# Two attention blocks, a gated MLP and a cross-attention with two norms, 16 batches: packing the heads tile to tile, affine parts of two norms at the transposes, new step orders

## What is computed

```
h  = x + attention(rmsnorm(x), rmsnorm(x))           # "sa": 16 heads of 16, keys 256
h  = h + attention(rmsnorm(h), ctx)                  # "ca": 16 heads of 16, keys 77
h3 = h + (silu(hn @ gate) * (hn @ up)) @ down        # "mlp", inner width 1024, hn = rmsnorm(h)
F  = layernorm(h3)*norm2_w + norm2_b                 # "nf", eps 1e-5
X  = layernorm(ctx)*norm1_w + norm1_b                # "nx"
xf = softmax(F X^T / 16) X, then a gelu MLP of width 4 -> cross
Cn = layernorm(cross)*norm3_w + norm3_b              # "nc"
out = F + gamma2 * (cross + gamma1 * softmax(Cn Cn^T / 16) Cn)
```

## Time and profile before

| what | before |
|---|---|
| median of 3 runs | 1182.13 us (1177.20 to 1184.93) |
| the profiled execution | 1181.4 us, span 1179.5 us |
| mean granted TensorE clock, share of full speed | 0.918 |
| PE busy | 1016.8 us (86%) |
| DVE, ACT, POOL busy | 664.5, 600.7, 320.8 us (56, 51, 27%) |
| one exponential step on ACT, 128x1024 (L624) | 1023 ns |
| one maxima step on DVE, 128x1024 (L753) | 1220 ns |
| ACT copy of a 128x512 transpose (L660) | 589 ns |
| ACT activation of 128x256 (L645) | 381 ns |
| POOL 128x256 (L500) | 731 ns |
| packing DMAs of sa, issue to landing: `scr_q`, `scr_k` / `qpk`, `kpk` of 256 KB | 3.0, 3.9 / 4.5, 7.4 us |

### The profile page before, as it was taken

One profiled execution on the slowest core, in us unless ns is written; L12 is line 12 of the kernel. 1 busy time (PEld: TensorE's weight loads), 2 busy tenths in 40 slices (PEclk: granted clock), 3 DMA queues, 4 the chain that ended last, 5 costly groups with the idle time before them and its releaser, 6 DMA issues.

```text
span 1179.5 us, 23087 instructions
## 1 busy us (share of the span) xinstructions
PE 1016.8 (86%) x8556; PEld 829.8 (70%) x8556; DVE 664.5 (56%) x1507; ACT 600.7 (51%) x1268; POOL 320.8 (27%) x460
## 2 busy tenths in 40 slices
PE   4264879899999999999999999999999999988854
PEld 3233557687777877877878777877778778776742
DVE  2524254556757585857565766667575758454421
ACT  3241435465655656463656565656556564744321
POOL 1000001022424242322323232424242423242442
PEclk9566679799999999998999999999999999998975
DMA  4503343434343515152433434443434251221000
GB/s 163 124 31 83 80 92 83 94 82 96 91 95 70 117 46 132 37 127 33 104 76 91 92 90 95 91 95 90 96 69 117 53 113 41 56 52 22 13 9 9
DMA packets 65975, 92.86 MB, mean 79 GB/s; under 512 B 15680, under 2 KB 59109, under 8 KB 61160
## 3 DMA queue, kind: packets, MB, share of 16 engines
q1 hardware_dynamic: 65896, 91.80, 33.7%
HBM read 58.81 MB, written 32.96 MB: 78 GB/s over the span
## 4 chain that ended last, share of the span: by engine, by line
PE 69%; DVE 10%; DMA 7%; ACT 6%; issue 4%; SPq 2%; POOL 2%; DVEq 0%; POOLq 0%; ACTq 0%
PE ring L901 16%; PE mring L901 13%; PE od L992 8%; DVE mx_sa L753 7%; PE ring L958 6%; PE ring L978 5%; PE down_ps L1042 4%; PE mring L1115 3%; DMA kpk_sa<-scr_k_sa 3%; PE mring L1103 3%; ACT probs L624 3%; PE ring L1004 2%; PE mring L1052 2%; PE mring L1091 2%; PE mring L1069 1%
## 5 line engine op out<-in xcount | busy, mean ns | idle before, releaser
L624 ACT ACTIVATE probs<-ring 128x1024 f32<-128x1024 f32 (+1 forms) x192 | 190.3, 1023 | 17.5 <-PE ring L978 14.5
L500 POOL TENSOR_TENSOR hidT_lo<-hid,hidT_hi 128x256 fp32r<-128x256 f32 x128 | 93.6, 731 | 353.5 <-ACT hidT_hi L653 353.5
L753 DVE TENSOR_REDUCE mx_sa<-ring 128x4 f32<-128x1024 f32 x128 | 153.9, 1220 | 38.1 <-PE ring L958 38.0
L958 PE MATMUL ring<-kpk_sa,qpk_sa 48*128 48x256 f32 x512 | 69.7, 362 | 56.6 <-DMA kpk_sa<-scr_k_sa 28.4
L958 PEld LDWEIGHTS ring<-kpk_sa,qpk_sa 48*128 48x128 f32 x512 | 43.4, 212 | 79.3 <-DVE mx_sa L753 37.5
L645 ACT ACTIVATE hid<-mring 128x256 f32<-128x256 f32 x128 | 48.8, 381 | 74.7 <-PE mring L901 73.1
L798 DVE SCALAR_TENSOR_TENSOR hid<-hid,mring 128x256 f32<-128x256 f32 x128 | 53.2, 416 | 50.8 <-ACT hid L645 50.4
L992 PE MATMUL od<-probs,vz_sa 128*32 128x256 f32 x1024 | 79.7, 417 | 2.4 <-ACT oS L632 2.4
L1042 PE MATMUL down_ps<-down_hi,hidT_hi 128*128 128x256 f32 x256 | 81.7, 319 | 0.0
L660 ACT ACTIVATE l_buf<-mring 128x512 f32<-128x512 f32 x64 | 37.7, 589 | 84.2 <-PE mring L1052 81.1
L758 DVE TENSOR_REDUCE mx_ca<-ring 128x4 f32<-128x308 f32 x128 | 52.6, 473 | 38.5 <-PE ring L958 38.5
(11 more groups left out here) (222 smaller groups left out, 2727.0 us busy)
## 6 DMA issues: line engine op xcount, KB each, us to landing
scr_q_sa<-qT SPq DMA_DIRECT2D x16, 512.0 KB, 3.0
scr_k_sa<-kT SPq DMA_DIRECT2D x16, 512.0 KB, 3.9
qpk_sa<-scr_q_sa SPq DMA_DIRECT2D x32, 256.0 KB, 4.5
kpk_sa<-scr_k_sa SPq DMA_DIRECT2D x32, 256.0 KB, 7.4
scr_q_ca<-qT SPq DMA_DIRECT2D x16, 512.0 KB, 3.0
qpk_ca<-scr_q_ca SPq DMA_DIRECT2D x32, 256.0 KB, 4.5
x_sb<-x SPq DMA_DIRECT2D x16, 256.0 KB, 4.9
qpk_sa<-scr_q_sa SPq DMA_DIRECT2D x32, 128.0 KB, 5.0
```

Of the source, the lines that this page charges most:

```text
L500: nc.gpsimd.tensor_tensor(hidT[1][:, m % HID, :], hid[:, m % 2, :], hidT[0][:, m % HID, :].bitcast(F32), ALU.subtract).then_inc(S["hidlo"] ...
L624: nc.scalar.activation(granule(g, tag)[0:rows_, i0:i0 + 2, :, :].rearrange("p i h t -> p h i t"), ring_tile(("E", tag, k))[0:rows_].rearra ...
L753: nc.vector.tensor_reduce(mx[tag][:, :, :, k].rearrange("p q h -> p h q"), ps[:].rearrange("p h (q t) -> p h q t", t=T), AX_X, ALU.max).th ...
L958: last = mm(ps[:, half, col:col + kw], qpk[tag][r, slot, q * P:(q + 1) * P], kpk[tag][r, slot, :], start=True, stop=True)
```

## The change

- The scratch tensors go. `pack_q` (step `pq`) and `pack_k` (`pk`) copy straight from `qT` and `kT` to `qpk` and `kpk`, six DMAs each, 16 partitions x 8 x 256 at a time (8 x 78 for the k of ca); the tile `qT` gives 128 partitions of 1 KB to each. `max_rows` (`mr`) copies `mT` straight to the two rows, in two DMAs.
- `qT` and `kT` come free when the packing has landed (`pqk`, now 192 = 12 times 16), not when the scratch is written; the wait for the last use of `qpk` by the batch before moves from SP to DVE's `qk`.
- `nf` and `nc` are transposed as centred tiles, and ACT applies weight and bias at the emptying, in two activations (`affine`) where there was one copy. POOL keeps the powers (`lnstat`), loses `lncen` (eight instructions of 128x256 a batch) and `out` (six), and gets `bF` and `bC`, two instructions of 128x512 each, which make `nF`\*norm2_w plus a bias row plus gamma2\*`cross`; DVE gets one addition of 128x512 (`out`, L857). The last product now takes the centred `nC`, and its weight and bias are folded into rows of constants (three POOL instructions at the start, once).
- All five lists of `ORDER` are new. FIRST and LAST, which set the loop, stay as they were.

```diff
-        scr_q = {t: nc.dram_tensor(f"scr_q_{t}", (C, 2, P, T), F32, kind="Internal").ap() for t in KW}
...
-            def pack_in(n, tag):
-                if not_first(n):
-                    sp.wait_ge(S[tag, "E"].sem, S[tag, "E"].at(n - 1, 8 if tag == "sa" else 4))
...
+            def pack_q(n, tag):
+                sp.wait_ge(S[tag, "qklo"].sem, S[tag, "qklo"].at(n, 1))
+                for half in range(2):
+                    for j, part in enumerate((0, 1, 0)):
+                        r = 64 * half + HD * j
+                        sp.dma_start(qpk[tag][r:r + HD].bitcast(F32), qT[:, half, part, :].bitcast(F32)).then_inc(S[tag, "pqk"].sem, 16)
+            def pack_k(n, tag):
...
+                sp.wait_ge(S[tag, "qklo"].sem, S[tag, "qklo"].at(n, 2))
+                for half in range(2):
+                    for j, part in enumerate((0, 0, 1)):
+                        r = 64 * half + HD * j
+                        sp.dma_start(kpk[tag][r:r + HD].bitcast(F32), kT[tag][:, half, part, :].bitcast(F32)).then_inc(S[tag, "pqk"].sem, 16)
+            def max_rows(n, tag):
+                sp.wait_ge(S[tag, "mT"].sem, S[tag, "mT"].at(n, 1))
...
+                    sp.dma_start(qpk[tag][r:r + 2].bitcast(F32), mT[2 * SLOTS * half:2 * SLOTS * (half + 1), :].bitcast(F32)).then_inc(S[tag, "mr"].sem, 16)
...
             def qk(n, tag):
+                if not_first(n):
+                    dve.wait_ge(S[tag, "E"].sem, S[tag, "E"].at(n - 1, 8 if tag == "sa" else 4))
...
-                    nc.gpsimd.tensor_tensor(NRM[tag][:, q, :], NRM[tag][:, q, :], bc[0:r, at_row, :], ALU.mult).then_inc(S[tag, "scl"].sem, 1)
...
+                nc.gpsimd.tensor_tensor(nF[:], nF[:], row("n2w"), ALU.mult).then_inc(S["base"].sem, 1)
+                nc.gpsimd.tensor_tensor(nF[:], nF[:], row("n2b"), ALU.add).then_inc(S["base"].sem, 1)
...
+                nc.gpsimd.tensor_tensor(cross[:], cross[:], row("g2"), ALU.mult).then_inc(S["base"].sem, 1)
+                nc.gpsimd.tensor_tensor(nF[:], nF[:], cross[:], ALU.add).then_inc(S["base"].sem, 1)
...
+                    for c in range(C):
+                        nc.scalar.activation(dst[:, c, :], mring_tile((fill,))[:, c * cols:(c + 1) * cols], ACT.Identity,
+                                             bias=normw[:, AFFINE_AT[tag] + 1, c:c + 1], scale=normw[:, AFFINE_AT[tag], c:c + 1]).then_inc(S[fill].sem, 1)
...
+            def out_(n):
+                dve.wait_ge(S["base"].sem, S["base"].at(n, 4))
...
+                nc.vector.tensor_tensor(o_sb[:], t1[:], nF[:], ALU.add).then_inc(S["o"].sem, 1)
...
-        E.sa.4@1 sc@-2 E.sa.5@1 pv.sa.1@1 E.sa.6@1 gu.4@-1 gu.5@-1 E.sa.7@1 dnp.2@-1 pT@-2 S.ca.0@0 S.ca.1@0 h4@-2 pv.sa.2@1 S.ca.2@0 S.ca.3@0 pv.sa.3@1
+        gu.3@-1 nFT@-2 dnp.1@-1 E.sa.2@1 E.sa.3@1 pv.sa.0@1 sc@-2 E.sa.4@1 gu.4@-1 E.sa.5@1 S.ca.0@0 pv.sa.1@1 gu.5@-1 S.ca.1@0 E.sa.6@1 pv.sa.2@1 pT@-2
```

More of the change, by code:

```diff
@@ L458, in pack_in @@
[L458 to L463, removed]
@@ L477, in _ @@
+            run(sp, "sp", {"wl": load_w, "ldx": load_x, "ldr": load_res, "ldc": load_ctx, "ldcl": load_ctx_l, "st": store, "pq": pack_q, "pk": pack_k, "mr": max_rows})
             sp.wait_ge(stored.sem, stored.at(B - 1, 16))
@@ L532, in _ @@
+            pool.wait_ge(s_bc, 2)
+            nc.gpsimd.tensor_tensor(bc[:, 4, :], bc[:, 4, :], bc[:, 5, :], ALU.mult).then_inc(s_fold, 1)
+            pool.wait_ge(s_fold, 1)
+            nc.gpsimd.tensor_tensor(bc[:, 2:4, :], bc[:, 2:4, :], bc[:, 4, :].unsqueeze(1).to_broadcast([P, QT, D]), ALU.mult).then_inc(s_fold, 1)
+            pool.wait_ge(s_fold, 2)
+            nc.gpsimd.tensor_tensor(bc[:, 1, :], bc[:, 1, :], bc[:, 3, :], ALU.add).then_inc(s_fold, 1)
             pool.wait_ge(s_vset, 1)
-            run(pool, "pool", {"ms": rstds, "hi": hid_lo, "lnstat": lnstat, "lncen": lncen, "out": out_})
+            row = lambda name: bc[:, ROWS.index(name), :].unsqueeze(1).to_broadcast([P, QT, D])
@@ L536, in _ @@
+            run(pool, "pool", {"ms": rstds, "hi": hid_lo, "lnstat": lnstat, "bF": base_F, "bC": base_cross})
         @block.scalar
@@ L661, in evacuate, with affine, f @@
                 return f
-            def nXT_affine(n):
-                act.wait_ge(S["nXTmm"].sem, S["nXTmm"].at(n, 1))
-                if not_first(n):
-                    act.wait_ge(S["scmm"].sem, S["scmm"].at(n - 1, 1))
-                for c in range(C):
-                    nc.scalar.activation(nXT[:, c, :], mring_tile(("nXT",))[:, c * SKV:(c + 1) * SKV], ACT.Identity,
-                                         bias=normw[:, 4, c:c + 1], scale=normw[:, 3, c:c + 1]).then_inc(S["nXT"].sem, 1)
+            def affine(fill, tag, dst, cols, after):
+                def f(n):
+                    act.wait_ge(S[f"{fill}mm"].sem, S[f"{fill}mm"].at(n, 1))
+                    if after and not_first(n):
+                        act.wait_ge(S[after].sem, S[after].at(n - 1, 1))
+                    for c in range(C):
+                        nc.scalar.activation(dst[:, c, :], mring_tile((fill,))[:, c * cols:(c + 1) * cols], ACT.Identity,
+                                             bias=normw[:, AFFINE_AT[tag] + 1, c:c + 1], scale=normw[:, AFFINE_AT[tag], c:c + 1]).then_inc(S[fill].sem, 1)
+                return f
             def sce(n):
```

153 lines of the change are left out of this document (62 added, 91 removed).

## The result

The changed kernel took 1213.28 us (median of 4 runs, 1203.60 to 1222.19) beside 1182.49 for the kernel before. The highest of the four is counted as a slow run, and the ratio, 1.024 with an interval of 1.015 to 1.033, is of the other three, whose median is 1208.21. It is slower, by 28 us by the ratio and 31 by the median of all four; 1202, 21 more than before, was forecast. The profiled execution has a span of 1216.3 us. Its line 950 is line 958 of before, 738 is 753, 605 is 624, 817 is 832.

A forecast was written before the change was run, and what follows sets the result against it. PE's work was taken to bound the steady part (59.9 of 62.5 us a period), with packing as long as its cover. Steady +28.8, filling +5, emptying -13 make +20.8 on 1181.4: 1202 us, range 1132 to 1226.

The forecast's parts named there:

- What bounds it, and the packing: Steady part: PE's work bounds, packing as long as its cover; new packing 16.3 us for sa, 11.3 for ca.
- Cover and waits: Between qk and scores: cover falls to 15.1 us (sa) and 11.2 (ca), so PE waits 2.9 and 1.8 us.
- Steady period: Twelve periods in the middle: PE's work 59.9 us plus waits makes 64.9 instead of 62.5 each, +28.8 us.
- Filling: Start of the run: four exposed sa packings +6.4 us, row maxima -2, earlier S.ca +0.6, together +5 us.
- Emptying: End of the run: bias additions and last out steps leave the chain of norms, together -13 us.
- B: Packing copies bound by issue, twelve in 7.3 us; no steady packing wait, whole 1132 us; chance 0.15.
- C: Neighbouring packing copies overlap, packing 12.2 us and within its cover, whole 1143 us; chance 0.13.
- D: Packing waits only replace PE's 2.6 us of idle time, period stays 62.5 us, whole 1173 us; chance 0.17.

The follow-up runs named there:

- old_order_direct: Kernel before with its lists, weights and biases kept; only packing and row maxima go tile to tile: 1181.25 us, ratio 0.997 to the kernel before.
- old_gu6_ahead: All of the change but its lists, with gu.6 moved ahead of qk.sa on PE, ACT and DVE: 1199.59 us, ratio 1.014 to the kernel before.
- old_order_both: All of the change but its lists, in the order of the kernel before with the fewest moves needed: 1169.43 us, ratio 0.987 to the kernel before.
- short_copies: Changed kernel, but from the second batch on each packing copy moves only 16 of 256 columns: 1142.05 us, ratio 0.964 to the kernel before.
- cover_a: Changed kernel with gu.6 moved behind qk.sa and, on PE, S.ca.0 behind pv.sa.1: 1160.11 us, ratio 0.981 to the kernel before.

## Why the prediction held, and where it was off

The direction and the mechanism held: PE waits for the two packings because their cover shrank. The time came out near partly by luck, as the steady period shows.

**What bounds it, and the packing.** The reading that the packing was as long as its cover held: with the cover of before the copies brought no wait (old_order_direct), and 1.36 us less of it brought waits of 1.1 us (old_gu6_ahead). The duration, 16.3 us forecast, is 15.0: the rate to sixteen partitions is 122 GB/s, and the half-microsecond window I used showed 115, which I had rounded up to 1.2 us a copy. A sixteenth of the bytes removed the waits, and two queues at once moved no more, so it is bytes and not issue or pieces. That the sixteen destination partitions set the rate rests on the earlier trace rows; no copy from tile to tile with more of them was run. For ca 11.3 was forecast and 10.7 measured.

**Cover and waits.** 2.9 us were forecast for sa and 1.8 for ca; 1.5 and 1.3 came. Most of the difference for sa is the packing's 1.3 us.

**Steady period.** 64.9 forecast, 64.84 measured, and that is luck: three errors cancelled. The waits are 1.9 us less than forecast; the idle time that was said to vanish, 2.3 of 2.6 us, shrank by half, to 1.3 (45.4 less 30.8, over eleven); and PE's work, which was to stay the same, grew by 0.9 us a period, 0.6 of it by the clock, for which I had taken 0. The clock was the step with a wrong value: it costs 6.9 us of 26.2 here, and in old_gu6_ahead, with 13.7, more than the waits themselves.

**Filling.** +5 forecast, +17.0 in the profiled run and +11.6 in the second one. This is the term that was mis-sized. I counted the four open packings of sa, which together did not get longer (28.4 us before, 28.9 after), and left out that batches three and four already run like steady ones, with less cover and at a low clock: their periods were 70.6 and 70.0 us against 61.6 and 66.0. Two things make up most of it. The first are waits for the packing of ca, for which I had 0.6; PE's waits in the filling before and then after:

```profile
PE ring L958 <- DMA kpk_ca<-scr_k_ca: 2.8, 2, 2.5
```

```profile
PE ring L950 <- DMA kpk_ca<-kT: 9.1, 3, 4.8
```

The second is PE's busy time, 215.1 us against 205.6 for about as many matmuls. Busy time times one minus the granted clock, added up over the one-microsecond windows of the filling, is 50.8 against 40.0: the clock accounts for all of it. Giving back cover took the filling to 291.4, with 5.2 us of ca waits and 36.0 by the clock.

**Emptying.** -13 forecast, -6.4 and -9.2 measured, and -11.6 with the parts in the old order. The bias additions are gone from the chain as said. But the packing of ca lies open here too. PE's waits for it in the emptying are 2.6 us before, 0.6 in old_order_both, and with the new lists:

```profile
PE ring L950 <- DMA kpk_ca<-kT: 5.5, 2, 4.0
```

The 2.9 us more were in no term. Nor is POOL's new work hidden there. The chain's end after:

```profile
1195.76 0.70 POOL nc_rs L490
1196.48 2.69 DVE l_buf L817 x2
1199.22 1.13 PE mring L1044 x4
...
1213.05 0.69 DVE o_sb L857
```

The centring of `nc` takes 2.69 us for two instructions that took 0.74 before. POOL's timeline says what ran beside it:

```profile
1196.41 1.26 POOL L495 TENSOR_TENSOR l_buf<-l_buf,bc 128x512 f32<-128x512 f32 x1
1197.75 1.26 POOL L497 TENSOR_TENSOR l_buf<-l_buf,bc 128x512 f32<-128x512 f32 x1
```

`bF` of the last batch starts as soon as `nc_rs` is done, and DVE is slow until it ends: 1.95 us on the chain. The same 2.69 stands in old_order_both, and in the changed kernel the centring of `nf` at 1181.31, with POOL idle beside it, takes 0.75. `bF` ahead of `nc_rs` in POOL's list might avoid it; that wasn't tried. These two, 4.9 us, are most of what is missing from the 13 in the profiled run.

**The rivals.** B asked for a copy below 0.95 us; it is 1.07, and its floor of 7.3 us for twelve was too low, since issue is 0.64 each and not 0.45: 9.0 to 10.1. C wanted a packing of 12.2 us and falls with the 15.0; D falls with the period of 64.84 and again with old_gu6_ahead. What B and C said of the period without waits, 61.2, was near: 60.7.

The filling varies by 5 us between the two executions of the changed kernel with the clock: PE is busy 215.1 and 209.5 us for the same 1556 matmuls, of which the clock cost 50.8 and 45.0, while the waits for copies are the same (28.9 and 28.6 for sa, 9.1 and 9.0 for ca). Open is why the clock stays low for longer in one of them.

## What to carry to other kernels

A transfer that fills its cover exactly is a limit though no wait is listed for it: before new orders are taken, write down for each such transfer its length and the work that stands in front of its reader. In this kernel a wait of 1.1 to 1.8 us in PE's stream was followed in nine of 22 cases by 1.7 us lost to the clock, so it can cost twice its length, while waits of at most half a microsecond (short_copies) cost no clock. And where a change has a part in the code and a part in the order, time each alone: here the code gave 1.3%, the order took 3.7, and two moved steps gave 4.2 back.

## What was not expected of the hardware

- Dips of the clock follow single waits: nine stretches of 3 to 4 us at 0.50 after 22 waits of 1.4 us in the mean and 1.8 at most, none where the longest single wait was 0.85 us (cover_a). Which of the 22 is followed by one no view shows: one of 1.73 us was not, one of 1.12 was. Length alone does not decide, for before, two waits of up to 0.9 us for maxima in a period were followed by them too, in four of eleven periods.
- SBUF-to-SBUF copies to sixteen partitions ran at 122 GB/s with pieces of 1 KB, a DRAM read with pieces of 8 KB at 115 in the window of the earlier trace rows: no cost of the shorter pieces shows in the rate. Issue of one on SP takes 0.64 us, against 0.45 for a DRAM read.
- With two 128x512 instructions on POOL beside them, two 128x256 instructions on DVE took 2.69 us instead of 0.74.
